# A fused attention and FP4 feed-forward kernel: the down product one step later, h quantized whole, and the output added to the stored x1 by an accumulating transfer

## The reference, cut to what matters

```python
x = x + xattn(layernorm(x), ctx, ctx, mask, Wq, bq, Wk, bk, Wv, bv, Wo, bo)
n = layernorm(x)
h = silu(fp4_linear(n, w_gate)) * fp4_linear(n, w_up)
x = x + fp4_linear(h, w_down)
```

## Time and profile before

| | |
|---|---|
| time, median of 3 runs | 2188.06 us (2186.34 to 2188.51) |
| profiled execution, its own time | 2190.24 us |
| its span from the first to the last instruction | 2188.5 us |
| TensorE busy | 1954.9 us, 89% |
| VectorE busy | 1884.1 us, 86% |
| ScalarE busy | 1191.9 us, 54% |
| GpSimd busy | 395.2 us, 18% |
| DMA queue of SP | 247.67 MB, 51.3% of the 16 engines' span |
| mean granted TensorE clock | 0.961 of full |

### The profile page before, as it was taken

The page is one execution under the profiler, slowest core; times in us unless marked ns, Lnnn a source line. Parts: engine busy times, 40 slices in busy tenths (PEclk is TensorE's granted clock), DMA queues, the critical chain, the costliest instruction groups (busy, mean ns, idle before and its releaser), DMA issues.

```text
span 2188.5 us, 63466 instructions
## 1 busy us (share of the span) xinstructions
PE 1954.9 (89%) x24768; PEld 1228.0 (56%) x24960; DVE 1884.1 (86%) x3188; ACT 1191.9 (54%) x2617; POOL 395.2 (18%) x523
## 2 busy tenths in 40 slices
PE   6334899999998999999998999999999999999987
PEld 4222556666565656665565566665655566665654
DVE  7767889898987898988987898989888898988975
ACT  4534556655664566555664566556654566556631
POOL 4543111111111111111111111111111111111100
PEclk9656999999999999999999999999999999999999
DMA  5322665555555555555545555555545555555543
GB/s 168 80 68 64 106 125 126 115 114 115 124 113 107 122 124 118 118 108 127 121 98 122 121 127 115 113 115 124 123 102 122 122 127 117 111 118 121 121 90 63
DMA packets 663013, 248.19 MB, mean 113 GB/s; under 512 B 614870, under 2 KB 615894, under 8 KB 662974
## 3 DMA queue, kind: packets, MB, share of 16 engines
q1 hardware_dynamic: 661390, 247.67, 51.3%
q10 hardware_dynamic: 1584, 0.01, 0.0%
HBM read 65.97 MB, written 34.82 MB: 46 GB/s over the span
## 4 chain that ended last, share of the span: by engine, by line
DVE 23%; PE 19%; issue 18%; DMA 12%; ACT 12%; POOL 9%; SPq 7%; another core or an unknown queue 1%; ACTq 0%; POOLq 0%; DVEq 0%
PE psum L539 13%; DMA ph_room<-h_room 11%; SPq L353 5%; DVE h_room L895 4%; PE psum L630 4%; DVE neg_max L1054 4%; ACT L771 3%; DVE p_h L863 3%; POOL ln_rstd L507 3%; ACT silu_g L771 2%; POOL ln_var_eps L505 2%; ACT io_room L811 2%; ACT p_h L784 2%; POOL h_room L480 2%; DVE ln_stats L1018 2%
## 5 line engine op out<-in xcount | busy, mean ns | idle before, releaser
L610 PE MATMUL psum<-wguT,t_room 128*128 128x352 bf16 x6144 | 947.9, 313 | 4.5 <-DVE h_room L1048 1.1
L610 PEld LDWEIGHTS psum<-wguT,t_room 128*128 128x128 bf16 x6144 | 598.3, 98 | 327.8 <-DVE h_room L1048 2.0
L539 PE MATMUL psum<-wdT,ph_room 128*128 128x512 bf16 x1985 | 469.3, 385 | 84.5 <-DMA ph_room<-h_room 80.6
L539 PEld LDWEIGHTS psum<-wdT,ph_room 128*128 128x128 bf16 x2112 | 203.8, 99 | 336.5 <-DMA ph_room<-h_room 103.4
L505 POOL TENSOR_TENSOR ln_var_eps<-ln_mean_var,eps 128x1 f32<-128x1 f32 x128 | 64.5, 504 | 1618.7 <-DVE ln_mean_var L1020 1077.0
L702 ACT ACTIVATE h_sq<-h_room 128x640 bf16<-128x640 f32 (+3 forms) x158 | 121.1, 767 | 247.1 <-DVE h_room L895 247.1
L777 ACT ACTIVATE probs<-psum,neg_max 128x77 f32<-128x77 f32 x1024 | 235.0, 350 | 11.2 <-DVE neg_max L1054 10.4
L539 PE MATMUL psum<-t_room,wqT 128*128 128x128 bf16 x3072 | 188.3, 222 | 2.3 <-issue 1.0
L771 ACT ACTIVATE silu_g<-psum 128x352 f32<-128x352 f32 x256 | 117.3, 458 | 119.9 <-PE psum L610 119.2
L539 PEld LDWEIGHTS psum<-t_room,wqT 128*128 128x128 bf16 x3072 | 178.2, 100 | 7.2 <-issue 1.4
L539 PE MATMUL psum<-woT,t_room 128*128 128x512 bf16 x704 | 165.8, 385 | 14.5 <-issue 9.7
(11 more groups left out here) (100 smaller groups left out, 2471.5 us busy)
## 6 DMA issues: line engine op xcount, KB each, us to landing
io_room<-in_x_dram SPq DMA_DIRECT2D x128, 256.0 KB, 2.7
x_scratch<-x_new SPq DMA_DIRECT2D x64, 256.0 KB, 2.0
x_cur<-x_scratch SPq DMA_DIRECT2D x64, 256.0 KB, 3.4
out_dram<-io_room SPq DMA_DIRECT2D x64, 256.0 KB, 2.7
t_room<-halves SPq DMA_TRANSPOSE x192, 3.1
raw<-in_L_ffn_w_down_dram SPq DMA_DIRECT2D x4, 704.0 KB, 4.4
raw<-in_L_ffn_w_gate_dram SPq DMA_DIRECT2D x11, 256.0 KB, 2.7
raw<-in_L_ffn_w_up_dram SPq DMA_DIRECT2D x11, 256.0 KB, 3.0
```

Of the source, the lines that this page charges most:

```text
L539: ins = pe.matmul(dst, left(i), right(j), start=first and n == 0, stop=last and n == len(PRODUCTS) - 1)
L610: ins = pe.matmul(ps[:, 0:CW], xqT[:, i, kc, :], wguT[:, which, j, kc, cols], start=(kc == 0 and i == j), stop=(kc == KC - 1 and i == LO))
```

## The change

h is quantized in one piece, a step after it was made: all passes are over 1408 columns, with one cast, one low half, one transpose and one down product of 33 matmuls. That product belongs to tile e now, a step later than before, and stands before chunk 1. VectorE's `tile_out` is gone. ScalarE copies the down product from PSUM to `out_sb`. SP stores x1 straight into the output tensor, and GpSimd issues a transfer that adds `out_sb` to it in DRAM. `x1_scratch`, `x1_cur` and the load between them are gone. The order on all engines is rewritten: SP issues x_in, mask, x1's store and the transposes in another order, with x1's store and h's transpose at the end of the step; GpSimd's addition of bo also waits for the high half of q; ScalarE makes the output copy after the second high half of the probabilities; VectorE's second norm and its quantization of h are interleaved in another way. The 77 keys are split 26 + 26 + 25 in place of 32 + 32 + 13, so that the passes over the probabilities are 624 wide in place of 768 (`KN`), and the rest of `p_h` is set to zero once in the beginning.

```diff
-    KW = KJ * DK
+    KN = -(-KEYS // KJ)
+    KW = KJ * KN
```

SP, all of its order after the o transpose, the values and the keys:

```diff
+                if n is not None:
+                    probabilities(0)
+                if m is not None and existing(m + 1) is not None:
+                    after(xn_ready, m + 1)
+                    sp.dma_start(x_in, one(x_t, m + 1)).then_inc(x_loaded, 16)
...
+                    probabilities(1)
...
+                    after(x1_done, a + 1)
+                    sp.dma_start(one(out_t, a), x1_new[:]).then_inc(x1_stored, 16)
...
+                if d is not None:
+                    after(h_lo, d + 1)
+                    after(down_done, d)
+                    transposed(hT.rearrange("p s k t -> p (s k) t"), h_h.rearrange("p s w -> p (s w)"), hT_loaded)
```

GpSimd:

```diff
+            own.did(pool.memset(p_h[:].rearrange("p a s j w -> p (a s j w)").bitcast(U32), 0))
...
                     pool.wait_ge(xr_loaded, 16 * a + 16)
+                    if n is not None:
+                        pool.wait_ge(qT_hi, n + 1)
                     own.did(pool.tensor_tensor(xb, xb, bo_all[:], ALU.add), xb_ready, a + 1)
...
+                if e is not None:
+                    pool.wait_ge(x1_stored, 16 * e + 16)
+                    pool.wait_ge(out_ready, e + 1)
+                    pool.dma_start((out_t[bass.ds(e, 1)]).rearrange("a p d -> (a p) d"), out_sb, accum_op=ALU.add)\
+                        .then_inc(out_stored, 16)
```

TensorE, behind the output projection:

```diff
+                if e is not None:
+                    pe.wait_ge(hT_loaded, 16 * e + 16)
+                    at_least(pe, out_ready, e)
+                    for k in range(IC):
+                        ins = split_product(down_ps, lambda s: hT[:, s, k, :], lambda s: wdT[:, s, k, :],
+                                            k == 0, k == IC - 1)
+                    ins.then_inc(down_done, 1)
```

```diff
+                if e is not None:
+                    act.wait_ge(down_done, e + 1)
+                    at_least(act, out_stored, 16 * e)
+                    act.copy(out_sb, down_ps).then_inc(out_ready, 1)
```

VectorE, the order of a step afterwards (weave points left out):

```diff
                 run(a, normalised)
                 run(m, first_norm)
+                run(a, half_low, o_h, o_sb, o_hi, o_lo, a)
+                run(d, top, hj, (h_done, d * CHUNKS + CHUNKS) if d is not None else None)
+                run(m, first_norm_end)
                 run(n, q_low)
+                run(d, scale, hj)
+                run(d, inverse, hj)
                 run(n, maximum, 0)
+                run(d, divide, hj)
                 run(n, maximum, 1)
                 run(a, residual)
                 run(a, second_norm)
+                run(f, h_chunk, 0)
+                run(a, second_norm_end)
+                run(d, first_round, hj)
+                run(d, second_round, hj)
+                run(d, rescale, hj)
+                run(a, top, xj, (xn2_ready, a + 1) if a is not None else None)
+                run(a, scale, xj)
+                run(a, inverse, xj)
+                run(n, probabilities_low, 0)
+                run(m, half_low, xn_h, xn, xn_hi, xn_lo, m)
+                run(a, divide, xj)
+                run(n, probabilities_low, 1)
+                run(f, h_chunk, 1)
                 run(a, first_round, xj)
                 run(a, second_round, xj)
                 run(a, rescale, xj)
+                run(d, half_low, h_h, hq, h_hi, h_lo, d)
                 run(f, h_chunk, 2)
                 run(a, half_low, xq_h, xq, xq_hi, xq_lo, a)
                 run(f, h_chunk, 3)
```

More of the change, by code:

```diff
@@ L90, in xattn_fp4_ffn_kernel @@
     h_fills = [range(c, min(c + 4, IC)) for c in range(0, IC, 4)]
-    H_KS = [range(0, 2 * CW // P), range(2 * CW // P, IC)]
-    H_PARTS = [slice(ks.start * P, ks.stop * P) for ks in H_KS]
     x_t = x.rearrange("b (t p) d -> (b t) p d", p=P)
@@ L357, in step, with probabilities @@
                 n = existing(n)
+                def probabilities(pair):
+                    after(p_lo[pair], n + 1)
+                    after(pv_done, GH * n)
+                    transposed(pT[:, pair].rearrange("p s j g t -> p (s j g) t"),
+                               p_h[:, pair].rearrange("p s j w -> p (s j w)"), pT_loaded[pair])
                 weave("norm")
@@ L820, in step @@
                     exponentials(0, range(GROUPS))
+                weave("scores")
+                if d is not None:
+                    square(h_sq[:], hv, h_val, d + 1, h_square)
+                if n is not None:
                     act.wait_ge(s_max, 2 * n + 2)
                     exponentials(1, range(2)).then_inc(exp_done, 1)
-                    probabilities_high(0)
-                    exponentials(1, range(2, GROUPS)).then_inc(exp_done, 1)
-                weave("scores")
-                if d is not None:
-                    act.wait_ge(hB_ready, d + 1)
-                    at_least(act, hB_loaded, 16 * d)
-                    act.copy(h_h[1][:, HI], hq[:, H_PARTS[1]]).then_inc(hB_hi, 1)
+                if m is not None:
+                    act.wait_ge(ln1_rstd, m + 1)
+                    at_least(act, xn_lo, m)
+                    act.activation(xn, x_in, ACT.Identity, bias=ln1_shift, scale=ln1_rstd_sb)\
+                       .then_inc(xn_ready, 1)
+                    act.wait_ge(xn_ready, m + 1)
+                    at_least(act, xnT_loaded, 16 * m)
+                    act.copy(xn_h[:, HI], xn).then_inc(xn_hi, 1)
+                weave("first")
                 if a is not None:
@@ L1017, in first_norm, with first_norm_end @@
                     dve.wait_ge(x_loaded, 16 * m + 16)
-                    own.did(dve.bn_stats(ln1_stats_sb, x_in))
-                    own.after()
+                    marks["norm1"] = own.did(dve.bn_stats(ln1_stats_sb, x_in))
+                def first_norm_end():
+                    own.after(marks["norm1"])
                     own.did(dve.bn_aggr(ln1_mean_var, ln1_stats_sb), ln1_stats, m + 1)
@@ L1121, in step @@
                 weave("end")
-                run(f, top, ha, (h_done, f * CHUNKS + 2) if f is not None else None)
-                run(f, scales, ha)
-                run(f, divide, ha)
+                run(d, half_low, h_h, hq, h_hi, h_lo, d)
                 run(f, h_chunk, 2)
                 run(a, half_low, xq_h, xq, xq_hi, xq_lo, a)
-                run(f, first_round, ha)
-                run(f, second_round, ha)
-                run(f, rescale, ha)
                 run(f, h_chunk, 3)
-                run(f, half_low, h_h[0], hq[:, H_PARTS[0]], hA_hi, hA_lo, f)
                 own.restart()
```

181 lines of the change are left out of this document (56 added, 125 removed).

## The result

The changed kernel takes 2224.67 us (median of 4 runs, 2221.39 to 2225.85), against 2188.27 for the kernel before in the same comparison: a ratio of 1.0166, 95% interval 1.0148 to 1.0184. The forecast was 2171, with a range to 2204. It is slower by 36 us where 17 us of gain were forecast; direction and range are both wrong.

What follows compares the result with a forecast made beforehand. TensorE's work, 29.49 us of a 30.49 us step, plus a 1.00 us transpose wait was taken as the bound. Savings of 31.3 and 3 less 17 in the tail took 2188.06 to 2171 us; own range 2158 to 2183, full range 2133 to 2204.

Steps and rivals of the forecast that it cites:

- What bounded the kernel before: Steady step of 30.49 us: TensorE works all but 1.00 us, waiting for the transpose of h's second part; floor 29.49.
- the boundaries: At three batch boundaries twelve value loads delay h's transpose, TensorE stands 5.42 us; most of 20.6 us excess, expected to go.
- The chain through the engines: New order through VectorE, GpSimd and ScalarE sets the step: 30.30 us, 0.19 less than before.
- silu 1's end: ScalarE's path from 18.90 us, through norm, exponentials, copies and table load, was summed to end at 25.48 us.
- The queues just fit: SP's transposes land in time: second p transpose out 24.95, landed 28.8; xq's out 30.95, landed 34.0, wanted 34.3.
- rival (2): Chain 0.5 us a step longer, xq's transpose landing in 3.9 instead of 3.1: 2200 us; chance 0.22, including slow GpSimd issue.
- The tail: End of the kernel, after the last steps: quantizing h whole and the later down product lose together 17 us.
- Its chain of 19.9: At the end, last h chunk to its transpose in use, h whole: 19.9 us against 13.1, +6.8.
- its 33 matmuls of 10.1: Last down product, 33 matmuls in place of 18, some 14 at half clock: 10.1 us against 6.8, +3.3.
- The last chunk: Last tile's chunk ends some 5 us later: down product before chunk 1 (4.0) and xq's transpose no longer covered (1 to 2).
- the way out: At the end, output copy, issue and landing of the accumulating transfer: 5.1 us against 3.3, +1.8.
- The sum: Whole kernel: steps and boundaries save 31.3 us, first four steps 3, tail loses 17; net -17.3 us.

Runs made afterwards that it cites:

- e4_both: Changed kernel with x1's store and the next x's load issued early and the accumulating transfer one step later: 2188.94 us, ratio 1.0005.
- e6: e5 with h's transpose issued on SP behind the attention output's transpose of the next step: 2177.97 us, ratio 0.9960.
- e9: e4_both with the down product's copy moved from ScalarE to VectorE: 2159.55 us, ratio 0.9875.
- e8: e2 without accumulating transfer: x1 through a scratch tensor, added by VectorE, output stored by SP a step later: 2146.98 us, ratio 0.9815.
- e14: Changed kernel with only the down product's copy moved from ScalarE to VectorE: 2370.21 us, ratio 1.0837.
- e5: e4_both with VectorE waiting for the second norm ahead of its three passes over h: 2144.75 us, ratio 0.9796.
- e13: Changed kernel with only VectorE's wait for the second norm ahead of its three passes over h: 2254.34 us, ratio 1.0313.
- e3: Changed kernel with the accumulating transfer issued one step later, behind GpSimd's addition to xb: 2193.78 us, ratio 1.0027.
- e2: Changed kernel with x1's store and the next x's load issued right after x1 is ready: 2196.48 us, ratio 1.0040.
- e10: Changed kernel with a plain store by GpSimd at the accumulating transfer's place, nothing added: 2199.61 us, ratio 1.0056.

## Why the prediction was wrong, step by step

**What bounded the kernel before, and the boundaries:** right. The wait of 1.00 us and the boundary stands went: e4_both has no step above 31.1 us from the fifth to the 61st, where the kernel before has three of 34.1 to 37.8.

**The chain through the engines:** right where nothing was late ahead of it. In e4_both the scores end at 8.83, the first maximum starts at 8.96 and the second ends at 12.00, all as forecast; GpSimd's three instructions end 0.14 behind the last pass. Then the residual comes 0.5 late and the step is 30.51 instead of 30.30. One sum is written wrong: silu 1's end, from the terms as they stand, is 25.37 and not 25.48, a tenth that would have made the forecast some 6 us lower. The missed term is SP's issue of the whole h's transpose: I took its landing (5.9; it is 5.2 to 5.4) and not its issue, 3.3 us for 2 x 1408 columns, with the attention output's transpose queued behind it. 0.21 x 58 = 12 us. The timeline shows this term; the one run that takes it away (e6) makes h's own transpose late instead.

**"The queues just fit": this step failed.** The second p transpose was to be out at 24.95 and landed at 28.8, with 1.5 us of room. It is out at 25.66, since the x load and the mask load are issued ahead of it, and lands after 5.1 instead of 3.8, at 30.8; the next value product follows at 31.02. I had named the accumulating transfer beside it and called it covered by that room. The transpose of xq was to be out 0.65 behind the value product and landed at 3.7, wanted at 4.0. It is out at 0.44 and lands after 3.8, at 4.3. Together 1925.3 - 1889.1 = 36.2 us over the 62 steps, by e4_both. This was rival (2), with its mechanism, its place and its 3.1 turning into 3.8; it was priced at 2200 because it had one late transpose where there are two.

**The tail:** 25.1 instead of 17. Its chain of 19.9 is 20.0 (2186.36 to 2206.36), its 33 matmuls of 10.1 are 9.58. Two terms were too small. The last chunk ends 10.9 later than before, not 5: the last tile's chunk 0 waits 3.48 for xq's transpose and then runs mostly at the 1.2 GHz level (granted clock 0.56), 6.58 us instead of 3.75. And the way out takes 8.0 us from the last matmul's end instead of 5.1: copy 0.59, 0.54 until GpSimd issues, and 6.8 from the issue to the end of the program, where 1.0 + 3.4 were taken. Before it was 3.5, so this part lost 4.5; e9 against e8 gives much the same by itself, 4.9 us more at the end than with a store by SP.

**The sum:** forecast -34.3 in the steps and +17 in the tail. Measured -4.0 ahead of the first step (not forecast, and its cause stays open), +14.3 in the steps, +25.1 in the tail. Of the 48.6 us in the steps, 36.2 are the late transposes, by e4_both, and the 12.4 that are left are put down to the issue of h's transpose.

**Left open:** why a transpose lands after 5.1 us when a transfer is issued 1.0 us ahead of it and after 7.0 when they are issued together; the runs show the order, not the cause. SP's issue alone isn't it: it takes 0.8 us longer than usual in the changed kernel (2.28), but not in e14 (1.46), where the landing is latest. What a split of h's quantisation in the last tile alone would give back of the tail was not tried.

## What to carry to other kernels

A transpose on which TensorE waits has a price that depends on what is issued beside it: read the room behind each landing as a sum (when the queue gets to issue it, landing beside the traffic of that moment, the wake-up), and before an engine's chain is shortened, look whether the next thing to come is a queue. SP's issue time belongs to a transfer as much as its landing. Where one small instruction of GpSimd is awaited, try letting VectorE stand for it ahead of its long passes: 1.3 us of idle time a step gave 44 us with the transfers moved away (e5 against e4), but cost 30 us with them in place (e13 against the changed kernel).

## What the runs showed of the hardware that was not expected

- 256 KB added into DRAM by GpSimd: 0.94 us of issue beside the transposes, 4.5 us to landing there (5.8 and 6.9 in e13 and e14) and 4.1 early in the step (e3, e4); a plain store by GpSimd at the crowded place 3.4, by SP 2.1 (e8) to 2.7 (before). The Trainium skill's figures for one transfer issued by GpSimd ("DMA: Bandwidth & Descriptors", section "Anatomy of one DMA"), 2.0 us and the bytes at 436 GB/s, make an estimate of 2.6 us. Both of GpSimd's transfers took longer here, the plain one by 0.8 and the accumulating one by 1.5 or more.
- A transpose of the same size landed after 3.8, 5.1, 5.3 or 7.0 us by the moment at which another engine's transfer was issued, and a kernel that differs only in the engine and the moment of one 0.6 us copy was 6.5% slower for it (e14 against the changed one).
- SP needs 3.3 us to issue a transpose of 2816 columns, 1.24 for 1024, and 1.4 to 1.5 for 1248; with a transfer of GpSimd 1.0 to 2.1 us ahead the last one took 2.2 to 2.6 (changed, e2, e10, e13).
